# The opening of a conv and attention kernel rearranged: 25 in place of 35 first-batch taps on TensorE, between the score steps

## The reference, cut to what matters

```python
qkv = concat(x @ wq.T, x @ wk.T, x @ wv.T)            # 768 channels
dw = conv5x5_depthwise(qkv); pw = conv1x1_grouped(dw)  # 25 taps per channel
query, key_, value = relu(q), relu(k), v               # of qkv and of pw, 8 channels a head
scores = einsum('bhdn,bhen->bhde', [value, 1], key_)
out = einsum('bhde,bhen->bhdn', scores, query)
out = out[:, :, :-1] / (out[:, :, -1:] + 1e-15)        # the last row is the denominator
x1 = batchnorm(conv1x1(out)) + x
F, G = conv1x1(norm(x1)); attention = softmax(F.T @ G)
y = conv1x1(conv1x1(x1) @ attention.T) + x1
```

## Time and profile before

| | us |
|---|---|
| median of three runs | 734.28 |
| the profiled execution | 734.32 |
| its span, first to last instruction | 732.5 |
| TensorE busy in the span | 666.1 (91%) |
| VectorE busy | 570.8 (78%) |
| GpSimd busy | 530.7 (72%) |
| ScalarE busy | 465.7 (64%) |
| mean granted TensorE clock | 0.965 of full |

### The profile page before, as it was taken

The page is one execution under the profiler, slowest core; times in us unless marked ns, Lnnn a source line. Parts: engine busy times, 40 slices in busy tenths (PEclk is TensorE's granted clock), DMA queues, the critical chain, the costliest instruction groups (busy, mean ns, idle before and its releaser), DMA issues.

```text
span 732.5 us, 8826 instructions
## 1 busy us (share of the span) xinstructions
PE 666.1 (91%) x3276; PEld 494.2 (67%) x3276; DVE 570.8 (78%) x669; ACT 465.7 (64%) x735; POOL 530.7 (72%) x248
## 2 busy tenths in 40 slices
PE   4979998999999999989989999899899956997998
PEld 3844456765777788655767887658687842475887
DVE  6999626998889999979889999888899992342231
ACT  3764443898867678797767867977686571232231
POOL 3449993989998999899989998899989782000000
PEclk9999997999999999999999999999999996899999
DMA  7000001000110000001100000000100000000000
GB/s 284 1 0 1 0 0 58 1 1 0 59 58 0 30 16 16 1 0 58 44 15 15 16 30 0 1 1 1 58 15 15 30 0 0 1 1 0 15 15 29
DMA packets 4938, 16.25 MB, mean 22 GB/s; under 512 B 800, under 2 KB 928, under 8 KB 3872
## 3 DMA queue, kind: packets, MB, share of 16 engines
q1 hardware_dynamic: 4896, 15.69, 5.8%
HBM read 11.50 MB, written 4.19 MB: 21 GB/s over the span
## 4 chain that ended last, share of the span: by engine, by line
PE 58%; ACT 16%; DVE 14%; POOL 7%; issue 3%; DMA 1%; SPq 0%; POOLq 0%; DVEq 0%; ACTq 0%
PE ps L585 12%; PE ps L561 11%; PE ps L495 8%; ACT prod L841 7%; POOL rows L1268 7%; DVE ps L1063 6%; PE ps L662 5%; PE ps L596 3%; PE ps L576 3%; DVE small L1200 2%; PE ps L448 2%; ACT kt L855 2%; PE ps L710 2%; PE ps L504 2%; ACT vt L856 2%
## 5 line engine op out<-in xcount | busy, mean ns | idle before, releaser
L1268 POOL TENSOR_TENSOR conv<-conv,prod 128x930 f32<-128x930 f32 (+4 forms) x192 | 422.6, 2232 | 40.8 <-ACT prod L841 37.3
L1063 DVE SCALAR_TENSOR_TENSOR ps<-raw,dw_sb,ps 128x960 f32<-128x960 f32 (+4 forms) x290 | 348.3, 1201 | 7.6
L841 ACT ACTIVATE prod<-raw,dw_sb 128x930 f32<-128x930 f32 (+4 forms) x228 | 247.3, 1138 | 35.1 <-POOL conv L1268 22.4
L585 PE MATMUL ps<-ht,pt 128*128 128x256 f32 x512 | 115.1, 379 | 0.0
L585 PEld LDWEIGHTS ps<-ht,pt 128*128 128x128 f32 x512 | 95.1, 190 | 11.8
L1268 POOL TENSOR_TENSOR rows<-rows,prod 128x930 f32<-128x930 f32 (+4 forms) x36 | 82.9, 2304 | 22.0 <-ACT prod L841 17.2
L984 ACT ACTIVATE rows<-ps,small 128x1024 f32<-128x1024 f32 x32 | 35.6, 1113 | 76.9 <-DVE small L1204 76.9
L1200 DVE TENSOR_REDUCE small<-ps 128x1 f32<-128x1024 f32 x32 | 39.1, 1221 | 33.0 <-PE ps L561 33.0
L561 PE MATMUL ps<-hi,t_hi 128*128 128x512 f32 x128 | 46.9, 449 | 13.1 <-ACT rows L984 13.1
L448 PE MATMUL ps<-hi,wqkv_hi 128*128 128x512 f32 x96 | 40.6, 423 | 11.3 <-DVE lo L350 10.2
L855 ACT ACTIVATE kt<-ps 128x256 f32<-128x256 f32 x68 | 31.7, 469 | 29.8 <-PE ps L618 26.5
(11 more groups left out here) (134 smaller groups left out, 1080.2 us busy)
## 6 DMA issues: line engine op xcount, KB each, us to landing
q_raw<-x_dram SPq DMA_DIRECT2D x4, 1024.0 KB, 6.4
x<-x_dram SPq DMA_DIRECT2D x4, 1024.0 KB, 4.8
out_dram<-x_t SPq DMA_DIRECT2D x16, 256.0 KB, 2.3
conv<-wqkv_dram SPq DMA_DIRECT2D x1, 768.0 KB, 4.5
conv<-fg_dram SPq DMA_DIRECT2D x1, 512.0 KB, 5.8
proj_sb<-proj_dram SPq DMA_DIRECT2D x1, 512.0 KB, 7.6
pw_sb<-pw_dram SPq DMA_DIRECT2D x1, 384.0 KB, 6.8
mask_sb<-masks_dram SPq DMA_DIRECT2D x1, 264.0 KB, 6.2
```

Source lines behind the costliest of these rows:

```text
L585: mm = pe.matmul(dst[:, 0:C], pt[:, i % PT_BUFS, j, :], ht[:, j, :], start=(j == 0), stop=(j == NB - 1))
L841: act.activation(dst, view, ACT.Copy, scale=weight(t, i)).then_inc(prod_ready, 1)
L1063: return dve.scalar_tensor_tensor(dst, view, w, before, ALU.mult, ALU.add)
L1268: pool.tensor_tensor(total, total, product, ALU.add).then_inc(conv_pool, 1)
```

## The change

It (1) loads each x in two halves with a semaphore each, and ScalarE starts on a half when it has landed; (2) lets TensorE begin the first raw tile with the products that need only `hi`; (3) orders the first batch's tiles 4, 2, 3, 5; (4) computes only tile 5's 25 taps on TensorE, in two halves, the second cut at taps 6, 12 and 18 with the score steps between the pieces; (5) gives tile 0's first ten taps back to VectorE, and takes tile 1's taps 17 to 21 in the first batch from VectorE to ScalarE and GpSimd (12 shared taps in place of 7); (6) moves the batch-norm steps from VectorE to ScalarE; (7) puts GpSimd's `split_lo(1)` after 29 adds in place of 4; (8) places VectorE's score steps between its taps (after indices 42, 51, 57 and 62); (9) sets ScalarE's product tables anew.

```diff
-SHARED_TAPS = 7
+SHARED_TAPS, FIRST_SHARED_TAPS = 7, 12
 KV_TILES = (2, 4, 5, 3)
+FIRST_KV_TILES = (4, 2, 3, 5)
-PE_TAPS = [(PE_TILE, i) for i in range(NTAPS)] + [(PE_SHARED_TILE, i) for i in range(PE_SHARED_TAPS)]
+PE_TAPS = [(PE_TILE, i) for i in range(NTAPS)]
-FIRST_TAPS = 64
+FIRST_TAPS = (42, 51, 57, 62)
+FIRST_SPLIT = 29
-FIRST_PRODUCTS_RAWKV = (0, 0, 0, 4, 0, 0, 0, 0)
-FIRST_PRODUCTS_KVT = (0, 1, 0, 0, 0, 2, 1, 1, 0)
-FIRST_PRODUCTS_RAWQ = (0, 1, 0, 0)
-FIRST_PRODUCTS_CONV = (13, 9, 13)
-FIRST_PRODUCTS_M = 22
+FIRST_PRODUCTS_RAWKV = (0, 3, 0, 1, 4, 0, 0, 0)
+FIRST_PRODUCTS_KVT = (2, 0, 0, 1, 2, 2, 0, 0, 0)
+FIRST_PRODUCTS_RAWQ = (1, 0, 0, 2)
+FIRST_PRODUCTS_CONV = (16, 0)
+FIRST_PRODUCTS_M = (3, 9, 15)
+CONV_BREAKS = (6, 12, 18)
-        a_end = lay_out(A_AT, [("raw_kv", A_RAWKV), ("kvt", A_KVT), ("raw_q", A_RAWQ), ("conv", A_CONV),
-                               ("conv_shared", A_CONV), ("st_raw", 1), ("mb_raw", 1)], 0, 0)
+        a_end = lay_out(A_AT, [("raw_kv", A_RAWKV), ("kvt", A_KVT), ("raw_q", A_RAWQ), ("conv_0", A_CONV),
+                               ("st_raw", 1), ("mb_raw", 1), ("conv_1", A_CONV)], 0, 0)
...
             def load_x(b):
-                sp.dma_start(q_raw[:, b % 2], x[b]).then_inc(x_loaded[b % 2], 16)
+                for h in range(2):
+                    cols = slice(h * HALF, (h + 1) * HALF)
+                    sp.dma_start(q_raw[:, b % 2, :, cols], x[b][:, :, cols]).then_inc(x_loaded[b % 2][h], 16)
...
+            def first_raw_tile():
+                t = FIRST_KV_TILES[0]
+                cols = [slice(h * HALF, (h + 1) * HALF) for h in range(2)]
+                dst = [a_slot(A_AT["raw_kv", 0] + h) for h in range(2)]
+                weights = [wqkv_hi[:, k, t * P:(t + 1) * P] for k in range(CK)]
+                pe.wait_ge(weights_hi, 1)
+                for h in range(2):
+                    pe.wait_ge(hi_ready, h + 1)
+                    for k in range(CK):
+                        pe.matmul(dst[h], weights[k], hi[:, k, cols[h]], start=(k == 0), stop=False)
+                pe.wait_ge(weights_lo, 1)
+                for h in range(2):
+                    for k in range(CK):
+                        pe.matmul(dst[h], wqkv_lo[:, k, t * P:(t + 1) * P], hi[:, k, cols[h]], start=False, stop=False)
+                for h in range(2):
+                    pe.wait_ge(lo_ready, h + 1)
+                    for k in range(CK):
+                        mm = pe.matmul(dst[h], weights[k], lo[:, k, cols[h]], start=False, stop=(k == CK - 1))
+                    mm.then_inc(a_full, 1)
...
-            def diagonal_conv(slot, t, taps):
+            def diagonal_conv(h, first, last):
+                bank = a_bank(conv_slot(h))
+                for i in range(first, last):
...
+                if last == NTAPS:
+                    mm.then_inc(a_full, A_CONV)
...
-            diagonal_conv(A_AT["conv", 0], PE_TILE, NTAPS)
-            diagonal_conv(A_AT["conv_shared", 0], PE_SHARED_TILE, PE_SHARED_TAPS)
+            diagonal_conv(0, 0, NTAPS)
             pe.wait_ge(vec_ready, 1)
             scores(D_AT["sc_raw", 0], A_AT["kvt", 0] + A_KVT, RB)
+            diagonal_conv(1, 0, CONV_BREAKS[0])
+            denominators(D_AT["den_raw", 0], D_AT["sc_raw", 0], q_raw[:, 0], A_AT["raw_q", 0] + A_RAWQ)
             score_transposes(A_AT["st_raw", 0], D_AT["sc_raw", 0])
-            denominators(D_AT["den_raw", 0], D_AT["sc_raw", 0], q_raw[:, 0], A_AT["raw_q", 0] + A_RAWQ)
+            diagonal_conv(1, CONV_BREAKS[0], CONV_BREAKS[1])
             fused_weights(A_AT["mb_raw", 0], A_AT["st_raw", 0], 0)
-            for h in range(CK):
-                spread_denominators(D_AT["bc_raw", 0], 1, h)
+            spread_denominators(D_AT["bc_raw", 0], 1, 0)
+            diagonal_conv(1, CONV_BREAKS[1], CONV_BREAKS[2])
+            spread_denominators(D_AT["bc_raw", 0], 1, 1)
+            diagonal_conv(1, CONV_BREAKS[2], NTAPS)
...
             products(FIRST_PRODUCTS_CONV[0])
-            diagonal_conv(A_AT["conv", 0], PE_TILE)
+            act.wait_ge(bn_rstd_ready, 1)
...
+            mm.then_inc(bn_ready, 1)
+            diagonal_conv(0)
             products(FIRST_PRODUCTS_CONV[1])
-            diagonal_conv(A_AT["conv_shared", 0], PE_SHARED_TILE)
-            products(FIRST_PRODUCTS_CONV[2])
             score_transposes(A_AT["st_raw", 0])
-            products(FIRST_PRODUCTS_M)
+            products(FIRST_PRODUCTS_M[0])
             fused_weights(A_AT["mb_raw", 0], 0)
+            products(FIRST_PRODUCTS_M[1])
+            diagonal_conv(1)
+            products(FIRST_PRODUCTS_M[2])
             products(PRODUCTS)
...
-            dve.wait_ge(bn_rstd_ready, 1)
-            step(dve.tensor_tensor(bn_scale, bn_tmp, gamma, ALU.mult))
-            step(dve.tensor_tensor(bn_tmp, bn_scale, mean, ALU.mult))
-            dve.tensor_tensor(bn_shift, beta, bn_tmp, ALU.subtract).then_inc(bn_ready, 1)
-            conv_taps(0, FIRST_WEIGHTS, FIRST_TAPS)
+            first_taps(FIRST_TAPS[0])
             scores(D_AT["sc_raw", 0])
+            first_taps(FIRST_TAPS[1])
             denominators(D_AT["den_raw", 0])
-            for t in range(CK):
-                scaled_queries(D_AT["bc_raw", 0], q_raw[:, 0], t)
-            conv_taps(0, FIRST_TAPS, DVE_TAPS - CARRY)
+            first_taps(FIRST_TAPS[2])
+            scaled_queries(D_AT["bc_raw", 0], q_raw[:, 0], 0)
+            first_taps(FIRST_TAPS[3])
+            scaled_queries(D_AT["bc_raw", 0], q_raw[:, 0], 1)
+            first_taps(DVE_TAPS)
...
-            conv_adds(0, 0, 4)
+            conv_adds(0, 0, FIRST_SPLIT)
             split_lo(pool, 1)
-            conv_adds(0, 4, POOL_ADDS)
+            conv_adds(0, FIRST_SPLIT, POOL_ADDS)
```

More of the change, by code:

```diff
@@ L53, with pool_order @@
 LATE = 10
-SHARED_TAPS = 7
+SHARED_TAPS, FIRST_SHARED_TAPS = 7, 12
 PROD_BUFS = 5
 KV_TILES = (2, 4, 5, 3)
+FIRST_KV_TILES = (4, 2, 3, 5)
 Q_TILES = (0, 1)
-PE_TILE, PE_SHARED_TILE = 5, 0
-PE_SHARED_TAPS = 10
-PE_TAPS = [(PE_TILE, i) for i in range(NTAPS)] + [(PE_SHARED_TILE, i) for i in range(PE_SHARED_TAPS)]
-PE_SHARED_END = (PE_SHARED_TILE, PE_SHARED_TAPS)
+PE_TILE = 5
+PE_TAPS = [(PE_TILE, i) for i in range(NTAPS)]
 SHARED_AT = 32
 CARRY = 16
-def pool_order(taps):
+def pool_order(taps, shared=SHARED_TAPS):
     own = [(t, i) for i in range(NTAPS) for t in POOL_TILES]
-    for i in range(SHARED_TAPS):
+    for i in range(shared):
         own.insert(SHARED_AT + 2 * i, (SHARED_TILE, LATE + i))
@@ L83 @@
 POOL_SEQ = pool_order(ALL_TAPS)
-FIRST_POOL_SEQ = pool_order([tap for tap in ALL_TAPS if tap not in PE_TAPS])
+FIRST_POOL_SEQ = pool_order([tap for tap in ALL_TAPS if tap not in PE_TAPS], FIRST_SHARED_TAPS)
 DVE_SEQ = [(t, i) for t in DVE_TILES for i in range(NTAPS) if (t, i) not in POOL_SEQ + LATE_SEQ]
@@ L227, in conv_seq_kernel @@
         w_loaded = sem("w_loaded")
-        x_loaded = [sem("x_even_loaded"), sem("x_odd_loaded")]
+        x_loaded = [[sem(f"x_{parity}_{half}_loaded") for half in ("left", "right")] for parity in ("even", "odd")]
         res_loaded = sem("res_loaded")
@@ L384, in diagonal @@
             n = PE_TAPS.index((t, i))
[L385 to L389, removed]
+            if n < 2 * NB:
+                return ht[:, n // 2, n % 2 * P:(n % 2 + 1) * P]
+            n -= 2 * NB
+            return x1[:, n // NB, n % NB * P:(n % NB + 1) * P]
         block = ctx.enter_context(nc.Block())
@@ L463, in raw_unit @@
                      hi[:, k, cols], lo[:, k, cols]) for k in range(CK)]).then_inc(a_full, 1)
+            def first_raw_tile():
[17 more added lines that the diff above has]
+                    mm.then_inc(a_full, 1)
             def raw_kv(b):
-                for u in range(A_RAWKV):
-                    raw_unit(b, A_AT["raw_kv", b] + u, KV_TILES, u)
+                for u in range(0 if b else 2, A_RAWKV):
+                    raw_unit(b, A_AT["raw_kv", b] + u, kv_tiles(b), u)
             def kv_transposes(b, j):
@@ L477, in kv_transposes @@
                 mm.then_inc(a_full, 1)
-            def diagonal_conv(slot, t, taps):
[L481 to L496, removed]
+            def diagonal_conv(h, first, last):
+                bank = a_bank(conv_slot(h))
+                for i in range(first, last):
+                    dst, view = square(bank), tap_view(PE_TILE, i)
+                    y0, y1 = h * SIDE // 2, (h + 1) * SIDE // 2
+                    if i > 0:
+                        dy, dx = shift(i)
+                        y0, y1 = max(y0, -dy), min(y1, SIDE - dy)
+                        x0, x_end = max(0, -dx), SIDE - max(0, dx)
+                        dst = dst[:, y0 - h * SIDE // 2:y1 - h * SIDE // 2, x0:x_end]
+                        view = view[:, y0:y1, x0:x_end]
+                    else:
+                        view = view[:, y0:y1, :]
+                    mm = pe.matmul(dst, diagonal(PE_TILE, i), view, start=(i == 0), stop=(i == NTAPS - 1))
+                if last == NTAPS:
+                    mm.then_inc(a_full, A_CONV)
```

(5 more changed lines are left out.)

45 lines of the change are left out of this document (34 added, 11 removed).

## The result

The changed kernel takes 716.54 us in the median of four runs (713.72 to 716.60), beside 734.0 for the kernel before in its four (731.80 to 736.58): ratio 0.9754, 95% interval 0.9726 to 0.9781. Forecast were 716.1, and 711.5 to 722.5. The profiled execution took 716.49 us with a span of 714.5.

A forecast was written before the change was run, and what follows sets the result against it. TensorE was taken to bound the opening, with GpSimd and VectorE ending within 1 us of it. 734.32 less body(0)'s earlier start (120.42 to 103.5) less 1.34 gave 716.1 us, 8-in-10 range 711.5 to 722.5.

The forecast's parts named there:

- E: Start of body(0) on TensorE, the end of the opening: forecast at 103.5 us in place of 120.42.
- the 1.34 us: Body(0), without its start at the half clock, should shorten by this much to body(1)'s 153.85 us.
- Front: Start of the opening: earlier hi from half loads and an earlier TensorE start gain 2.4 us, bounds 0 and 3.4.
- ScalarE: ScalarE up to raw q: six more products, 6.3 us, partly in idle time; raw q drained at 47.2, bounds 44 and 49.
- TensorE's first half: First half of tile 5's taps on TensorE: from 47.2 to 68.9, 21.7 us.
- GpSimd: GpSimd's adds in the opening: start at 16.0, 35 adds of 2.33 us plus one split, end at 102.3.
- rival (a): GpSimd bounds the opening, starting no sooner than 21.20 or starving: E 107.5, time 720.1; chance 0.14.
- VectorE: VectorE's chain in the opening: 5.6 us saved on batch-norm, scores from 73.2, denominators to 87.1, second scaled queries to 103.3.
- TensorE's last piece: Last seven taps on TensorE behind the second spread: 5.8 us, ending at 102.8.
- rival (b): Handovers add up: 1 us of waits and three clock falls of 1.1 us each; E 107.8, time 720.4; chance 0.15.
- Rival (c): The cut-up stretch on TensorE stays at half clock from the scores on: E 127, time 741; chance 0.07.
- a little: Margin at the opening's end: E set at 103.5, TensorE's last taps ending at 102.8.

The follow-up runs named there:

- the uncut run: Changed kernel with the second half of tile 5's taps on TensorE uncut, 24 taps right behind the scores and one at the end: 720.91 us, ratio 0.9800.
- one-load run: Changed kernel with each x loaded in one load again in place of two halves: 715.37 us.
- seven shared taps: Changed kernel with 7 shared taps of tile 1 in the first batch in place of 12: 716.17 us.
- split after 13: Changed kernel with GpSimd making the low part of x(1) after 13 adds in place of 29: 720.71 us.
- batch-norm run: Changed kernel with the three batch-norm steps back on VectorE in place of ScalarE: 716.0 us.
- the ten taps alone: Kernel before with only tile 0's ten taps moved back to VectorE, 25 taps on TensorE; score steps after index 64: 725.16 us, after index 50: 740.1.
- run with index 50: Kernel before with tile 0's ten taps back on VectorE and VectorE's score steps after index 50 of its list in place of 64: 740.1 us, ratio 1.0076.
- the one with 64: Kernel before with tile 0's ten taps back on VectorE and VectorE's score steps after index 64 as before: 725.16 us, ratio 0.9870.
- the refit with one load: Changed kernel with cuts at taps 6, 14, 22, 10 shared taps in place of 12, and each x in one load: 710.87 us, ratio 0.9677.
- the refit: Changed kernel with cuts at taps 6, 14, 22 in place of 6, 12, 18 and 10 shared taps in place of 12: 713.2 us, again 711.05.

## Why the prediction was right, and where it was not

**The frame held.** E and the length of body(0) were the two numbers to forecast: 103.5 and 153.85 against 103.34 and 153.85. That TensorE, busy up to E, starts body(0) at the full clock was the reason for the 1.34 us; the row at 103.34 has 48 matmuls in 5.52, and the uncut run, idle before E, has the slow start back and a body(0) of 154.74.

**Front: wrong.** The prediction had the first half of x land midway, `hi` at 6.8 and a gain of 2.4 us. `hi` began at 8.13, TensorE at 9.34 in place of 10.24; both units were copied at 15.5 in place of 16.2, so the gain was 0.7. The one-load run splits it: there both were copied by 14.35, so that the order of the first products alone brought 1.9, and the halves, in this pair of executions, took 1.2 back. The Trainium skill's rule to batch loads to 1 MiB or more (DMA: Bandwidth & Descriptors, Bandwidth), which I set aside, points the right way. My estimate from its 138 GB/s, 3.8 us for a half, did not come: that would have put the first half at 9.1, against 8.13 measured and 9.18 in the latest of eight executions, and its 2.6 us is the delay of the first half against 6.5, not of the whole.

**ScalarE: nearly, and TensorE's first half too long.** TensorE's first convolution matmul came at 48.18, forecast 47.2: of the 1.7 us that the front fell short, 1.0 reached it. The first half of the taps then took 20.1 us, not 21.7: the prediction added 1.1 us for a slow start that its mean of 0.414 already held, and here the clock did not fall at that start. So the scores ended 0.8 us early, at 72.3, and not late.

**GpSimd: right in the end by two errors.** It began at 17.75, not 16.0, and took 80.3 us for 35 adds, 2.30 each, not 2.33 or 81.6, ending at 102.63 against 102.3. My 2.33 leaves out the 0.48 us of idle time in the earlier trace rows, but the three adds behind it took 2.45 each, where the 23 ahead of it took 2.32; here 29 took 2.31 and the last six 2.23. But the claim that it bounds E along with the others failed: rival (a)'s engine has no say in E (seven shared taps), except through ScalarE's queue (split after 13).

**VectorE: right.** It started 1.6 us late, as tile 2 is now the second one (2.91 us of waiting), and that took the place of the 2.5 us it was to wait for scores; it reached them at 72.70 against 73.2. From there every step is within 1.1 us: denominators 84.29, second handover 93.53 (forecast 94.5), the last scaled queries to 102.2 (103.3).

**TensorE's last piece: mis-sized.** 5.8 us were forecast and 7.16 measured, because the clock fell in it. The same 14 matmuls took 5.50 at full clock in the batch-norm run, so the fall cost 1.7 us, which rival (b) priced at 1.1 each. One of its three falls came. Against the falls the prediction said that gaps stay under 2 us and that the trace shows a fall only after longer idle time. Its own rows spoke against that. In the earlier trace rows the second spread waits 1.48 us and takes 2.50, where the first, at 115.03, took 1.47. The window of TensorE in the kernel before has the clock at 0.50 there, and body(0) started slowly in the same fall:

```profile
118.00:119.00 1.00, 1.00 (x4) 0.50 1.06 451
```

Nor does the length of a wait decide by itself. In the changed kernel the clock fell after the wait of 1.95 us, 6.5 us behind another of 1.63, and stayed at 1.00 after one of 2.00 us that ended at 39.76. The Trainium skill (TensorE: Matmul & The Clock Gate, HAM oscillation) has the clock fall back between bursts of matmuls with waits between them; this trace agrees with it at one wait and not at the others. Rival (c) stayed away: the fall ended in three us.

**Luck in the sum.** E came within 0.2 us of the forecast by errors that cancel. The second spread ended at 96.34, not 97.0, 0.7 us early; the last piece, up to body(0), took 7.0 us, not 5.8, 1.2 late; and the 0.7 us that the prediction added as "a little" was not there. With the clock up, as the sum had it, TensorE would have been ready at about 101.7, and GpSimd's end at 102.63 would have come to bound E.

**What the decomposition shows.** Of the 17.8 us, the ten taps alone bring about 9.5 (725.16 to its 734.62), and there GpSimd's end at 111.8 is a floor, which the run with index 50 meets and the one with 64 ties with. The other parts bring the rest together. Two of them were taken out alone: without the cutting the kernel is 3.4 us slower by the ratios and 4.4 by the medians, with the split after 13 adds about 4 us. The earlier start of GpSimd was not taken out alone, so its share is argued. The parts do not simply add: taken out alone, the batch-norm steps, the loads and five of the twelve shared taps make no difference that the medians can show.

## What to carry to other kernels

When a stage ends in a handover chain between engines, write down each engine's finish line, not only the first: taking work off the bound engine made the kernel slower when the receiving engine was left standing at a wait with its work queued behind. Cut the filler work so that its pieces are as long as the waits between them, and leave as little as can be behind the last handover; here that was worth 3 to 5 us beyond the change. A pacing loop (products waiting for adds) makes every unrelated step queued behind it inherit the pace: look for what stands behind it before moving work on its far end.

## What the runs showed of the hardware that was not expected

**Two half loads landed later than one whole, and less regularly.** In eight executions with halves the first `hi` began at 7.35, 7.60, 8.13, 8.15, 8.45, 8.82, 8.95 and 9.18 us, the second some 1.3 us after it; in five with one load (the kernel before, the one-load run, the refit with one load, the ten taps with index 50 and 64) the whole began at 7.63 to 7.78. So the second half was always later than the whole, and the first in six of eight. A half has rows of 2 KB, 512 numbers, where the whole has rows of 8 KB; the page of the profile counts 6538 packets in place of 4938. The Trainium skill (DMA: Bandwidth & Descriptors, Bandwidth) asks for loads of 1 MiB and more; the runs agree in sign. Why the halves scatter over 1.8 us is open, and wasn't tried.

**Two-element operations on VectorE take 0.16 us, or wait until GpSimd's operation ends.** With GpSimd idle up to 46.50, in the run of the ten taps with index 50, the three batch-norm steps took:

```profile
46.09 0.15 DVE L1241 TENSOR_TENSOR small<-small,bn_sb 128x2 f32<-128x2 f32 x1
46.27 0.16 DVE L1242 TENSOR_TENSOR small<-small,bn_sb 128x2 f32<-128x2 f32 x1
46.47 0.16 DVE L1243 TENSOR_TENSOR small<-bn_sb,small 128x2 f32<-128x2 f32 x1
```

Beside its operations they took up to 2.28, the length of one of those, and ended with it: in the kernel before at 49.49, 51.81 and 53.88, where GpSimd's ended at 49.48, 51.79 and 53.86. In the run with index 64 the second and third took 2.30 and 2.27, ending at 48.64 and 50.95, GpSimd's at 48.62 and 50.93. The 0.16 us of the batch-norm run, at 51.09, fell between two adds, the one ending at 51.03 and the next beginning at 51.18.

The taps with the accumulator in PSUM do not feel it: 23 of them took 28.50 us with GpSimd mostly idle, and in the changed kernel, all of them beside its adds:

```profile
20.97 28.49 DVE L1107 SCALAR_TENSOR_TENSOR ps<-raw,dw_sb,ps 128x900 f32<-128x900 f32 x23
```

The tap that reads the accumulator from SBUF (`ps<-raw,dw_sb,conv`) does, at times: it took 1.29 us in the run with index 50, where it met no add, and 1.29 to 2.82 beside them in the openings of the other kernels. The Trainium skill (GPSIMD Engine Reference, Key points) states that VectorE and GpSimd share SBUF interfaces, with contention when VectorE's instruction has two SBUF inputs; these rows agree.

**A body is 152.3 or 153.85 us long, by whether TensorE's clock falls in it.** Body(1) of the changed kernel took 153.86 us and that of the run with seven shared taps 152.30. In both, some 94 us after its start, TensorE waits 1.53 us for ScalarE ahead of the energies. Behind that wait the clock fell for some three us in the first, not in the second. Changed kernel:

```profile
351.51 0.74 PE L590 MATMUL ps<-hi,t_hi 128*128 128x512 f32 x2 [1.53 <-ACT rows L1015]
...
353.00:354.00 1.00, 1.00 (x3) 0.50 0.00 0
```

Seven shared taps:

```profile
351.49 0.73 PE L590 MATMUL ps<-hi,t_hi 128*128 128x512 f32 x2 [1.53 <-ACT rows L1015]
...
353.00:354.00 1.00, 1.00 (x6) 1.00 0.00 0
```

Over the thirteen traces, the eight bodies of 152.6 us or less among bodies (0) to (2) have the clock at 1.00 throughout. The others have a fall in them or, body(0) of the refit in two runs, 1.8 us of waiting for VectorE. Why the same wait brings the fall in one execution and not in the next is open.
